# A fused cross-attention and mixture-of-experts block: a GpSimd wait at the second norm, an early Silu, and a new order of steps

## The reference

```python
x = x + tanh(g_xattn) * attention(layernorm(x), ctx)            # one head of 128, 512 keys
h = layernorm(x)
X = h
q, k, v = (rmsnorm(X, norm1_w) @ w for w in (wq, wk, wv))       # 16 heads of 8
X = X + softmax(q k^T / sqrt(8)) v @ wo                         # over 256 rows of the batch
h2 = rmsnorm(X, norm2_w)
logits = h2 @ router_w                                          # 8 experts, top 2, softmaxed weights
out = X + swiglu_shared(h2) + sum_e combine[:, e] * swiglu_e(h2)  # all 8 experts computed densely
x = x + tanh(g_ffn) * out
```

## Time and profile before

| | before |
|---|---|
| median of 3 runs | 225.95 us (222.45 to 226.83) |
| profiled execution | 221.48 us |
| its span, first to last instruction | 219.7 us |
| mean granted TensorE clock | 0.961 |
| busy: TensorE, VectorE, ScalarE, GpSimd | 195.8, 141.3, 103.3, 99.7 us |

### The profile page before, as it was taken

How to read it: one execution, slowest core, us unless ns; L and a number is a source line. 1 busy time by engine, 2 the same in 40 slices (tenths; PEclk the granted TensorE clock), 3 DMA queues, 4 the chain that set the end, 5 groups by cost and what they waited for, 6 DMA issues and landing times.

```text
span 219.7 us, 4544 instructions
## 1 busy us (share of the span) xinstructions
PE 195.8 (89%) x1575; PEld 170.6 (78%) x1575; DVE 141.3 (64%) x323; ACT 103.3 (47%) x219; POOL 99.7 (45%) x205
## 2 busy tenths in 40 slices
PE   7779867879959978898998999979999999999994
PEld 5467656758847756577886697969999999999993
DVE  3658556777765676566777265665887887564653
ACT  2396935614725846676676655322323325223220
POOL 2999950323054573476588880747182640000000
PEclk9999999967976999999999999997999999999999
DMA  5902298551579055964000000000000000000000
GB/s 174 309 16 48 51 166 143 90 84 34 65 92 131 18 123 70 108 110 145 4 3 0 3 0 0 4 0 3 24 0 4 0 25 3 0 3 24 0 4 24
DMA packets 9000, 11.56 MB, mean 53 GB/s; under 512 B 977, under 2 KB 6993, under 8 KB 8753
## 3 DMA queue, kind: packets, MB, share of 16 engines
q1 hardware_dynamic: 8976, 11.27, 27.5%
HBM read 5.50 MB, written 0.52 MB: 27 GB/s over the span
## 4 chain that ended last, share of the span: by engine, by line
PE 74%; DVE 11%; issue 5%; ACT 5%; POOL 3%; DMA 1%; SPq 0%; DVEq 0%; POOLq 0%; ACTq 0%
PE bank L1170 14%; PE bank L1160 8%; PE bank L1159 8%; PE bank L1158 8%; PE bank L1113 7%; PE bank L1141 7%; PE bank L1126 5%; PE bank L990 3%; DVE mxs L897 2%; PE bank L1005 2%; DVE xs L822 2%; PE bank L1022 2%; PE bank L1061 1%; DMA xs<-x_tiles 1%; PE bank L1076 1%
## 5 line engine op out<-in xcount | busy, mean ns | idle before, releaser
L897 DVE TENSOR_REDUCE mxs<-bank 128x2 f32<-128x512 f32 x64 | 42.5, 687 | 19.1 <-PE bank L1113 18.6
L724 ACT ACTIVATE ep<-bank 128x512 f32<-128x512 f32 x64 | 37.6, 601 | 23.5 <-PE bank L1126 23.1
L1158 PE MATMUL bank<-split,whi 128*128 128x256 f32 x144 | 43.5, 302 | 0.0
L1160 PE MATMUL bank<-split,wlo 128*128 128x256 f32 x144 | 41.1, 285 | 0.0
L1159 PE MATMUL bank<-split,whi 128*128 128x256 f32 x144 | 40.9, 284 | 0.0
L1170 PE MATMUL bank<-down_s,early 128*128 128x128 f32 x288 | 38.0, 275 | 0.1
L1170 PEld LDWEIGHTS bank<-down_s,early 128*128 128x128 f32 x288 | 35.3, 191 | 0.2 <-DVE early L917 0.2
L1113 PE MATMUL bank<-k_st,q_st 80*128 80x256 f32 x128 | 32.5, 343 | 2.0 <-DVE q_st L853 1.3
L1113 PEld LDWEIGHTS bank<-k_st,q_st 80*128 80x128 f32 x128 | 21.6, 209 | 8.6 <-issue 6.6
L1158 PEld LDWEIGHTS bank<-split,whi 128*128 128x128 f32 x144 | 27.9, 194 | 0.4 <-issue 0.4
L1159 PEld LDWEIGHTS bank<-split,whi 128*128 128x128 f32 x144 | 27.8, 193 | 0.0
(11 more groups left out here) (144 smaller groups left out, 314.4 us busy)
## 6 DMA issues: line engine op xcount, KB each, us to landing
raw<-expert_w SPq DMA_DIRECT2D x9, 256.0 KB, 7.1
k_st<-k_st SPq DMA_DIRECT2D x7, 256.0 KB, 5.4
q_st<-split SPq DMA_DIRECT2D x24, 64.0 KB
k_st<-split SPq DMA_DIRECT2D x24, 64.0 KB
down_s<-expert_w SPq DMA_DIRECT2D x9, 128.0 KB, 7.0
early<-ctx_T SPq DMA_DIRECT2D x1, 672.0 KB, 6.7
xs<-x_tiles SPq DMA_DIRECT2D x2, 256.0 KB, 3.9
out_dram<-x SPq DMA_DIRECT2D x4, 128.0 KB, 1.8
```

What stands on the lines that cost most here:

```text
L724: nc.scalar.activation(ep[:, n % NEP].rearrange("p t s -> p (t s)"), b_of(("exp", n))[:], ACT.Exp, scale=SCALE_H).then_inc(free(("exp", n) ...
L897: nc.vector.tensor_reduce(mxs[:, half % 2, :, 64 + h:65 + h], b_of(("max", n))[:].rearrange("p (t s) -> p t s", t=TB), AX_X, ALU.max).then ...
L1158: pe.matmul(bank, whi[:, fs], h2hi[:, hs], start=True, stop=False)
L1160: last = pe.matmul(bank, wlo[:, fs], h2hi[:, hs], start=False, stop=True)
```

## The change

1. GpSimd, which had nothing to do at step `n`, now waits there until VectorE has written the second norm's output of that batch (`hs_ready`).
2. ScalarE computes a Silu of one column into a new tile `silu_of`, ahead of the wait for the first item with Silu. The result isn't used. The table load goes with it.
3. `SEQ_STEPS`, `FIRST_STEPS` and `MIXED_STEPS` have new contents. The number of items inside the slots rises from 22 to 28.

```diff
-MIXED_STEPS = {0: "s5 y1", 2: "k1 xn3 o4 p5", 3: "e1", 4: "e2 o5 e3 n2 q3", 5: "h2 m0", 7: "s6", 8: "k2 p6",
+MIXED_STEPS = {0: "s5", 2: "k1 e1 p5", 3: "xn3 o4", 4: "o5 q3 e2 n2", 7: "m0 e3 h2 s6", 8: "k2 s7", 12: "y2",
...
         tg = sb("tg", [P, 2])
+        silu_of = sb("silu_of", [P, 1])
...
                 elif stage == "o" and i % TB == TB - 1:
                     norm2(i // TB)
+                elif stage == "n":
+
+                    pool.wait_ge(hs_ready, i + 1)
...
             def dense_up(n):
+                if n == len(tanh_items):
+
+                    nc.scalar.activation(silu_of[:], tg[:, 0:1], ACT.Silu)
                 is_full(act, ("gate", n))
```

More of the change, by code:

```diff
@@ L33 @@
 SEQ_STEPS = {
[3 rows of a table removed]
-        ("route_weights", 62, 63)],
[3 rows of a table removed]
-        ("route_weights", 58, 68)],
[3 rows of a table removed]
-        ("route_weights", 77, 80)],
[3 rows of a table removed]
-        ("route_weights", 115, 121)],
-}
-FIRST_STEPS = """f0 f1 g0 f2 xn0 q0 g1 s0 t0 s1 g2 p0 p1 f3 z0 r0 o0 xn1 xn2 o1 q1 s2 s3 y0 j0 q2 p2 g3 p3 n0 r1
-                 h0 o2 s4 o3 k0 n1 p4 e0 h1 w0""".split()
-MIXED_STEPS = {0: "s5 y1", 2: "k1 xn3 o4 p5", 3: "e1", 4: "e2 o5 e3 n2 q3", 5: "h2 m0", 7: "s6", 8: "k2 p6",
[5 rows of a table removed]
[3 rows of a table added]
+        ("route_weights", 60, 64)],
[3 rows of a table added]
+        ("route_weights", 66, 72)],
[3 rows of a table added]
+        ("route_weights", 82, 87)],
[3 rows of a table added]
+        ("route_weights", 118, 120)],
+}
+FIRST_STEPS = """f0 f1 g0 f2 t0 g1 xn0 q0 xn1 s0 g2 s1 p0 p1 z0 o0 f3 r0 o1 xn2 q1 s2 j0 s3 y0 n0 q2 p2 p3 g3 o2
+                 r1 h0 s4 o3 k0 y1 n1 w0 e0 p4 h1""".split()
+MIXED_STEPS = {0: "s5", 2: "k1 e1 p5", 3: "xn3 o4", 4: "o5 q3 e2 n2", 7: "m0 e3 h2 s6", 8: "k2 s7", 12: "y2",
[5 rows of a table added]
 BANKS = {"turn": (0, 1, 6), "proj": (2, 3, 7), "sum": (4, 5), "misc": (4, 5)}
```

## The result

| | before | after |
|---|---|---|
| median, runs of the first comparison | 224.2 us (220.74 to 226.83, 4 runs) | 214.6 us (214.38 to 216.79, 4 runs) |
| ratio, 95% interval | | 0.969 (0.963 to 0.975): faster |
| profiled execution, its span | 221.48, 219.7 us | 214.39, 212.5 us |
| mean granted clock | 0.961 | 1.000 |
| busy: TensorE, VectorE, ScalarE, GpSimd | 195.8, 141.3, 103.3, 99.7 us | 190.1, 139.8, 103.2, 99.7 us |

A forecast was written before the change was run, and what follows sets the result against it. Bound by TensorE (74% of the chain), with loss in its waits and half-clock stretches. 3.0 + 1.9 + 1.3 + 0.4 - 1.6 + 4.3 = 9.3 us off 221.48 gives 212.2; 1.8 added for run spread: 214.0 us, range 208.5 to 220.5.

The forecast's parts named there:

- Edit 1: GpSimd's wait at the second norm: VectorE's late pairs (batches 2, 3) take 0.61 instead of 2.13 us, 3.0 us won.
- Rest of the two waits: TensorE at the second norm's transposes, batches 2 and 3: the new order covers what the freed pairs leave, 1.9 us won.
- Third wait: TensorE's wait ahead of the matmuls at 38.00 for VectorE's stack copy goes because the stack moves earlier, 1.3 us won.
- The start: Batch 0's value projection fills part of the wait for the first split, 0.4 us won.
- New waits: Between the two late pairs VectorE sets the pace; TensorE waits for banks and batch 3's softmax, charged -1.6 us.
- Edit 2: The steps in a new order, giving TensorE more work ahead of the transposes; terms 1.9, 1.3, 0.4 and -1.6 us.
- The clock: Without waits above about 1 us, the first two half-clock stretches go: 4.3 us won; the third, around 148 us, stays.
- Rival B: Waits go but the clock falls anyway, as VectorE breaks up TensorE's work at 42 to 57 us: 216.5 us; chance 0.20.
- Attention's last group about 9 us earlier: Sign that the forecast is right: attention's last group comes about 9 us earlier than in the kernel before.
- Edit 3: The added one-element Silu ahead of the gate wins nothing and costs nothing, since the first Silu waits for TensorE.
- Rival F: Batch 0's pair is held by GpSimd's casts now beside it: about 1 us less gain, 215 us; chance 0.03.
- Rivals C and D: C (0.14): new waits replace the old, 223 us; D (0.05): work in pieces keeps the clock at half, about 233 us.

The follow-up runs named there:

- fill_gaps: The kernel before plus four throwaway TensorE matmuls ahead of its wait for the second norm's output, batches 2 and 3: 216.10 us, ratio 0.976.
- wait_m1: The kernel before with GpSimd's wait at step n, and m1 moved behind n3 in slot 16 of the old order: 212.92 us, ratio 0.962.
- wait_only: The kernel before with the GpSimd wait at step n and nothing else: 218.56 us, ratio 0.986.
- after_m1_first: The changed kernel with m1 (second expert's weight split) moved ahead of n3, so ahead of GpSimd's wait at batch 3: 214.87 us, ratio 0.971.
- wait_m1_e1: wait_m1 with step e1 (stacking batch 0's third and fourth queries) one slot earlier, in slot 2 behind k1: 213.2 us, ratio 0.959.
- e3_early: The changed kernel with step e3 (stacking batch 0's last four queries) in slot 5 instead of 7: 213.89 us, ratio 0.966.
- after_again: The changed kernel, unchanged, run again beside other kernels: 215.45 us (214.94 to 218.16).

## Why the prediction was right, and where it was not

The time, 214.6 us for 214.0, held, and so did the two largest terms of the mechanism: GpSimd's hold on VectorE and the clock. The sum behind the time did not: it gave 9.3 us off the profiled execution, and the trace has 7.1 (221.48 less 214.39). That the forecast came so near is luck: the 1.8 us that I added for the spread of runs was not needed, since with a clock that holds there is little spread, and made up for the 2.2 us that the sum had too much. By the spans of the four traces the 7.2 us are 5.8 for the clock (before to fill_gaps), 3.0 for the pairs (fill_gaps to wait_m1) and -1.6 for the new order (wait_m1 to after). Point by point:

- **Edit 1, 3.0 us: right.** The pairs took 0.61 us; 3.0 us between the spans of fill_gaps and wait_m1. But in the changed kernel only batch 2's place owes it to GpSimd's wait: wait_only shows that in the old order the wait alone doesn't reach batch 3, and after_m1_first that in the new one TensorE comes late enough there with the pair held.
- **Cost 0 for what stands behind the waiting GpSimd: no sign of another.** GpSimd idles 0.78 us; wait_m1, with both waits, has the gain in full.
- **Rest of the two waits, 1.9 us: right as waits.** L1020 has none; wait_m1, without the new order, keeps 1.9 us there.
- **Third wait, 1.3 us: failed.** The wait itself went, as the step "goes because that stack now stands ahead of two transposes and an output product" says. What the step left out is whose bank that output product (tile 4) gets. Banks go round in the order of use, and the new order has `p5` ahead of `o4`; so `o4` takes the bank of tile 5's turned probabilities, and waits until ScalarE has copied them. That copy (36.04) is queued behind the two casts of the moved stack. The copy that the product needs for its data had long run (30.94). ScalarE of after in order of time:

```profile
30.94 0.59 ACT L646 COPY early<-bank 128x512 f32<-128x512 f32 x1
...
34.84 0.58 ACT L670 CAST k_st<-bank 32x512 fp32r<-32x512 f32 x1 [0.31 <-PE bank L1042]
35.44 0.58 ACT L672 CAST k_st<-bank 32x512 fp32r<-32x512 f32 x1
36.04 0.59 ACT L646 COPY early<-bank 128x512 f32<-128x512 f32 x1
```

  So 1.07 us at 36.77 took the place of 1.31. wait_m1_e1, where the same stack is moved by itself, loses the wait and 1.3 us, although its casts stand ahead there too (34.56 and 35.16 us). Its `p5` is behind `o4`, and the product starts at once (TensorE of wait_m1_e1):

```profile
34.58 1.06 PE L1008 MATMUL bank<-early 128*128 128x128 f32 x8
```

  The moved casts alone make nobody wait. No run has the new order with `p5` behind `o4`, so what that would give back is not shown.
- **The start, 0.4 us: failed.** TensorE's first slot began at 31.17 us, before at 31.14.
- **New waits, -1.6 us: mis-sized.** I found pieces of 0.8, 1.0 and 0.6 us. The largest that came, 1.37 us for the bank of `e3`, is not among them; it alone costs 1.1 us (e3_early). "Here VectorE sets the pace" holds only in part: between the two pairs VectorE was busy 12.85 us, as I had counted (13), but the stretch took 16.80 us (after, the whole stretch):

```profile
42.44:59.24 16.80, 14.03 (x100) 10.79 (x100) 12.85 (x29) 8.93 (x20) 5.31 (x6) 1.00 0.57 79
```

  VectorE idled 3.95 us in it and TensorE 2.77, so each waited for the other in turn. With the terms above, the step "Edit 2" as a whole, 1.9 + 1.3 + 0.4 - 1.6 = +2.0 us, had the wrong sign: at full clock the new order is 1.8 us longer than the old with the same wait and `m1` behind it. Against wait_only, where `m1` stands ahead of the wait, the new order does bring 3.1 us (218.56 less 215.45); moving `m1` alone brings that and more. In the profiled executions of after and wait_m1 (spans 212.5 and 210.9 us) 0.8 us of the new order's loss lie ahead of attention's last group, which starts at 129.62 us in after and at 128.86 in wait_m1; the other 0.8 us comes behind it and I have not traced it to a step.
- **The clock, 4.3 us: right in kind, too small.** Both long stretches at half clock went, and so did the third, around 148 us, which I had left standing. Fillers alone bring 5.8 us, some 70% of the 8.1 us that the earlier trace rows allow at most (3.4 + 3.0 + 1.7). "No wait above about 1 us" is not the bound I took it for: after_again, with 1.37 us as its longest wait in that part, lost the clock in one execution of six badly enough to cost 2.5 us (183.8 us from the first slot to the end, for 181.3 in after). Rival B thus came true in a few executions and not in the median.
- **Attention's last group about 9 us earlier: no, 6.4** (136.02 to 129.62). From that group to the end the time fell from 83.7 us before to 82.1 in fill_gaps and 82.0 in wait_m1, where the third stretch at half clock is gone, and only to 82.9 with the new order.
- **Edit 3, 0 us: right.** The first Silu item starts 2.30 us after the item before, in after (190.55 less 188.25) as before, and waits for TensorE. The added Silu began 0.02 us behind the end of the load (188.86 + 1.28 = 190.14). The page "ScalarE: Activation LUTs" of the Trainium skill ("What ACT_TABLE_LOAD costs") has a drain of 1.38 us besides the load; this trace shows none at that place.
- **Six more Tanh items, hidden:** VectorE's busy time in 170 to 180 us is 7.98 us with TensorE at 10.00. Whether some of the 0.8 us behind attention is theirs was not tried.
- **Rival F: didn't come.** Batch 0's pair took 0.61 us at 20.36 us. The GpSimd work beside it turned out to be a memset, L495, not the casts, so what the casts would do is still unseen. The page "SBUF — State Buffer" of the Trainium skill ("SBUF: two separate sides") has a VectorE instruction with two SBUF inputs and a GpSimd instruction that reads SBUF exclude each other, and the one that comes second is blocked. I took from it that L417 would have held VectorE, and saw in the 0.61 us a sign against the page. I had looked at VectorE alone, and it was GpSimd that gave way: beside the pair at 28.89 us the first L418 of after took 1.06 us and the next, without it, 0.79, and in before the L417 that began at 20.65, beside L804 (20.50, the same kind of instruction) and the pair at 20.77, took 1.23 for 0.80. The pairs stayed at 0.62 and 0.61. So the traces agree that the two exclude each other. Only the split, L528 and L529, held VectorE here.
- **Rivals C and D: didn't come.** No wait of after for VectorE's maxima is above 0.8 us, and the clock rose again behind each fall. One number in D was wrong: "today's 12.8" us of half clock is TensorE's busy time in the first two stretches of the earlier trace rows, while the three together last 17.0 us. With that, 40 us of half clock would have cost 4.9 and not 7.0 us, and D would have decided from 39 us on and not from 35. The forecast doesn't hang on it.

## What to carry to other kernels

When an engine is to wait so that it doesn't disturb another, read its queue in order: the wait protects only what stands behind it, and here one pair of steps exchanged made the difference between 1.4% and 3.8%. Price the clock apart from the waiting, by giving TensorE throwaway work in the gap: that one run showed 5.8 us for the clock, of 8.8 us that the wait ahead of both splits gave in all (spans 219.7 and 210.9 us). When a step moves, follow not only the copy that someone waited for but also which bank each later step now gets and who reads that bank last; here a moved turn of the probabilities handed `o4` a bank that ScalarE was late with.

## What the runs showed of the hardware

- Clock and waiting are separate prices. Matmuls that compute nothing filled 3.6 of the 4.9 us that TensorE waited for the two pairs (1.3 were left) and made the kernel 5.8 us shorter, with the pairs as late as before. In the changed kernel the same matmuls cost 2.0 us.
- A wait does not settle the clock by itself. With equal instructions and equal waits up to the fall at 46 us, one execution of the changed kernel had 1.00 throughout and another 0.84 and 0.82 in two stretches, 214.39 and 218.16 us. What decides between them no run here shows.
- VectorE and GpSimd can hold each other, in either direction. A pair held by GpSimd is held twice over. Free, each of its two instructions takes 0.35 us. Beside L528 and L529 they took 0.79 and 1.42 us (wait_only, batch 3): the first ends behind the cast, the second behind the subtraction. Beside GpSimd's L417 and L418 the pairs stay at 0.61 and 0.62 us, and it is one GpSimd instruction that takes 1.06 to 1.23 us for 0.80.
